# Routing from unnormalised rows: centred router weights, the norm's scale after the choice, and each batch placed during the next one's output

## What is computed

```python
def _layernorm(x, axis=-1, eps=1e-05):
    return (x - mean(x)) / sqrt(var(x) + eps)

def _L1_ffn_ref(x, Wr, W1, W2):            # E = 8 experts, cap = 256 tokens each
    probs = softmax(xf @ Wr)
    eidx = argmax(probs);  p_tok = probs[eidx]
    rank = (how many earlier tokens chose the same expert);  keep = rank < cap
    h = maximum(xe @ W1[e], 0);  ye = (h @ W2[e]) * p_tok * keep
...
x = x + 0.5 * _L0_ffn_ref(_layernorm(x), ...)      # twice, an attention between
x = x + 0.5 * _L1_ffn_ref(_layernorm(x), ...)      # stage 0
x = x + _L1_attn_ref(_layernorm(x), ...)
x = x + 0.5 * _L1_ffn_ref(_layernorm(x), ...)      # stage 1
```

## Time and profile before

| | us |
|---|---|
| median of 3 runs | 621.57 (620.26 to 624.51) |
| profiled execution, device time | 621.04 |
| its span, first to last instruction | 619.2 |
| busy in that span: PE, DVE, POOL, ACT | 505.4, 342.3, 243.5, 214.8 |

### The profile page before, as it was taken

The page is one execution under the profiler, slowest core; times in us unless marked ns, Lnnn a source line. Parts: engine busy times, 40 slices in busy tenths (PEclk is TensorE's granted clock), DMA queues, the critical chain, the costliest instruction groups (busy, mean ns, idle before and its releaser), DMA issues.

```text
span 619.2 us, 10399 instructions
## 1 busy us (share of the span) xinstructions
PE 505.4 (82%) x3827; PEld 322.3 (52%) x3827; DVE 342.3 (55%) x912; ACT 214.8 (35%) x298; POOL 243.5 (39%) x292
## 2 busy tenths in 40 slices
PE   1787787989999999987888878965887788788893
PEld 0664333434644644462467744962456566563692
DVE  5654585648487757751144760323696888842131
ACT  1346331644455455445643701202231311110120
POOL 5667464223342334235332467452220220323153
PEclk9998797989999999998999999997998989977997
DMA  7306999733263263225299523312756273110220
GB/s 261 146 23 198 311 279 298 195 117 95 69 188 96 62 158 118 58 45 155 71 174 217 165 86 111 94 40 72 201 183 187 74 201 111 54 51 35 86 63 10
DMA packets 73666, 79.85 MB, mean 129 GB/s; under 512 B 10946, under 2 KB 50499, under 8 KB 73360
## 3 DMA queue, kind: packets, MB, share of 16 engines
q1 hardware_dynamic: 70760, 73.15, 42.6%
q0 software_dynamic: 2560, 5.58, 2.6%
q10 hardware_dynamic: 296, 0.47, 0.2%
HBM read 44.07 MB, written 35.72 MB: 129 GB/s over the span
## 4 chain that ended last, share of the span: by engine, by line
PE 49%; DVE 17%; SPq 8%; DMA 7%; POOL 7%; issue 6%; ACT 5%; POOLq 0%; DVEq 0%; ACTq 0%
PE ps_accum L1505 15%; PE ps_pair L1505 15%; PE ps_max_pair L1505 13%; SPq L366 3%; POOL sb_rstd L583 2%; DVE sb_stats L1061 2%; DVE sb_work L1400 2%; DMA sb_v_next<-v_scr 2%; DVE sb_mpart L1164 2%; SPq L380 1%; SPq L402 1%; PE ps_turn L1513 1%; POOL xe_scr L603 1%; PE ps_max_pair L1513 1%; DVE sb_mv L1064 1%
## 5 line engine op out<-in xcount | busy, mean ns | idle before, releaser
L1164 DVE TENSOR_REDUCE sb_mpart<-ps_max_pair 128x4 f32<-128x512 f32 x132 | 88.0, 688 | 47.1 <-PE ps_max_pair L1505 46.7
L900 ACT ACTIVATE sb_work<-ps_pair 128x1024 f32<-128x1024 f32 x80 | 80.9, 1024 | 71.3 <-PE ps_pair L1505 70.5
L1505 PE MATMUL ps_max_pair<-sb_ring,sb_m_sets 128*128 128x512 f32 x146 | 64.8, 471 | 7.6 <-DVE sb_mpart L1164 4.6
L660 POOL TENSOR_SCALAR_AFFINE_SELECT sb_work<-sb_work 128x512 f32<-128x512 f32 (+1 forms) x48 | 37.7, 789 | 72.1 <-ACT sb_work L900 72.1
L1505 PE MATMUL ps_pair<-sb_ring,sb_xsets 128*128 128x512 f32 x160 | 58.7, 455 | 8.9 <-DMA sb_ring<-sb_qs 3.7
L1505 PE MATMUL ps_pair<-sb_ident_bf,sb_ones_bf 128*128 128x512 bf16 x185 | 50.6, 431 | 12.3 <-DMA sb_x<-y_scr 8.0
L1505 PE MATMUL ps_accum<-sb_work,sb_v_aug 128*32 128x128 f32 (+3 forms) x768 | 59.3, 408 | 1.1 <-POOL sb_work L660 1.1
L1505 PEld LDWEIGHTS ps_max_pair<-sb_ring,sb_m_sets 128*128 128x128 f32 x146 | 26.9, 191 | 45.1 <-DVE sb_mpart L1164 28.7
L1505 PEld LDWEIGHTS ps_pair<-sb_ring,sb_xsets 128*128 128x128 f32 x160 | 29.0, 200 | 22.6 <-DMA sb_ring<-sb_qs 7.1
L1400 DVE TENSOR_TENSOR sb_work<-ps_pair,sb_cst 128x1024 f32<-128x1024 f32 x32 | 37.5, 1214 | 2.6 <-PE ps_pair L1505 2.6
L1505 PEld LDWEIGHTS ps_pair<-sb_ident_bf,sb_ones_bf 128*128 128x128 bf16 x185 | 19.9, 110 | 36.3 <-issue 11.7
(11 more groups left out here) (251 smaller groups left out, 994.6 us busy)
## 6 DMA issues: line engine op xcount, KB each, us to landing
sb_expert_rows<-xe_scr SPq DMA_DIRECT2D x16, 258.0 KB, 2.8
sb_m_sets<-q_scr SPq DMA_DIRECT2D x16, 256.0 KB
sb_ka_stk<-mk_scr SPq DMA_DIRECT2D x4, 1024.0 KB
xe_scr<-sb_cst SPq DMA_DIRECT2D x4, 1024.0 KB, 12.8
sb_mw<-in_mw SPq DMA_DIRECT2D x16, 256.0 KB, 5.9
sb_ka_stk<-mk_scr SPq DMA_DIRECT2D x8, 512.0 KB
sb_xsets<-k_scr SPq DMA_DIRECT2D x15, 256.0 KB
q_scr<-sb_qs SPq DMA_DIRECT2D x12, 256.0 KB, 3.7
```

The costliest lines, as they stand in the source:

```text
L660: pool.affine_select(weights, weights, [[0, weights.shape[1]], [0, HL], [1, P]], ALU.is_ge, 0.0, base=0, channel_multiplier=-1).then_inc(s ...
L900: act.activation(unit_slots(i), pair[u % 2][:], ACT.Exp, scale=SCALE).then_inc(s["exp_done"], 1)
L1164: dve.tensor_reduce(mpart[:, m // NPAIR, m % NPAIR, :], max_banks[m % 2][:].rearrange("p (h k) -> p h k", h=HL), AX.X, ALU.max).then_inc(s ...
L1505: return pe.matmul(dst, lhsT, rhs, start=start, stop=stop, skip_group_check=True)
```

## The change

The router's product is made on raw rows. Since the norm takes the mean off each row and multiplies by one positive number per row, `norm(x) @ Wr = rstd * (x @ (Wr - column means of Wr))`: the weights are centred once at the start, the choice is made on the unscaled logits, and only the Exp gets logits multiplied by rstd (`scaled_logits`). The placed rows still hold normed values. In stage 0 a batch's logits go behind the first quarter of the next batch's output and its ranks behind the third; DVE chooses and places a batch in the same `after_attention(b)`, so ahead of the next batch's add; POOL scatters one batch earlier than before. `place` is put in another order (what needs no ranks comes first; the same lines go from further down, which is not shown), and the one-hot's f32 copy counts the semaphore too. The unread products are set anew, and now a part of them waits until the scatters have landed.

POOL, stage 0:

```diff
-            for b in range(2):
+            rsqrt(norm_second(B), 0)
+            for b in range(1, B):
+                scatter(0, b - 1, 0, 2)
                 rsqrt(norm_second(B + b), b % 2)
-            for b in range(2, B):
-                scatter(0, b - 2, 0, 2)
-                rsqrt(norm_second(B + b), b % 2)
-                scatter(0, b - 2, 2, NT)
-            for b in range(B - 2, B):
-                scatter(0, b)
+                scatter(0, b - 1, 2, NT)
+            scatter(0, B - 1)
```

ACT:

```diff
             def router_exp(r):
-                act.wait_ge(s["lg_sub"], r + 1)
-                act.activation(r8[1][:], r8[0][:], ACT.Exp).then_inc(s["lg_exp"], 1)
+                act.wait_ge(s["lg_scaled"], r + 1)
+                act.activation(r8[1][:], r8[1][:], ACT.Exp).then_inc(s["lg_exp"], 1)
...
             def after_attention(b):
-                if b:
-                    turned_full(B + b - 1, turn[0], xnT[(b - 1) % 2][:])
                 if b + 1 < B:
                     gelu(B + b + 1)
+                turned_full(B + b, turn[1], xnT[b % 2][:])
                 if b + 2 < B:
                     turned_high(B + b + 2)
-                if b:
-                    router_exp(b - 1)
-                    if b + 2 < B:
-                        ready(ACT.Gelu)
+                router_exp(b)
+                if b + 2 < B:
+                    ready(ACT.Gelu)
```

DVE:

```diff
+            def scaled_logits(r, norm):
+
+                dve.wait_ge(s["rstd"], norm + 1)
+                dve.tensor_tensor(r8[1][:], r8[0][:], rstd[r % B % 2][:].unsqueeze(2).broadcast_to([P, NT, E]),
+                                  ALU.mult).then_inc(s["lg_scaled"], 1)
+
...
             def place(r, b, bank, places):
+                dve.wait_ge(s["top_onehot"], 2 * r + 2)
+                dve.tensor_tensor(r8[5][:].rearrange("p t e -> p (t e)"), r8[3][:].rearrange("p t e -> p (t e)"),
+                                  const("slot_base"), ALU.mult).then_inc(s["rank_c"], 1)
+                dve.tensor_scalar(rows_out[r // B][b][:, :, ID], spare[:], float(-NTOK), None, ALU.add)
+                dve.wait_ge(s["rank_c"], 2 * r + 1)
+                dve.tensor_reduce(r1[5][:], r8[5][:], AX.X, ALU.add).then_inc(s["rank_d"], 1)
+                dve.wait_ge(s["lg_exp"], r + 1)
+                dve.tensor_reduce(r1[2][:], r8[1][:], AX.X, ALU.add).then_inc(s["top_sum"], 1)
+                dve.wait_ge(s["top_sum"], r + 1)
+                dve.reciprocal(r1[3][:], r1[2][:]).then_inc(s["top_rcp"], 1)
                 dve.wait_ge(s["rank_mm"], r + 1)
...
             def after_attention(b):
                 old = rows_out[0][b][:, :, OLD:RW]
                 ffn_x(B + b, x[b], old)
-                moments(norm_second(B + b), old, b % 2)
-                if b:
-                    choose(b - 1, accum[1])
-                normalise(norm_second(B + b), old, rows_out[0][b], b % 2)
+                n = norm_second(B + b)
+                moments(n, old, b % 2)
+                choose(b, accum[1])
+                normalise(n, old, rows_out[0][b], b % 2)
+                scaled_logits(b, n)
                 if b + 2 < B:
                     low(B + b + 2)
-                if b:
-                    place(b - 1, b - 1, accum[1], slot_all[:, NT * (b - 1):NT * b])
+                place(b, b, accum[1], slot_all[:, NT * b:NT * (b + 1)])
...
+            dve.wait_ge(s["wr_sum"], 1)
+            dve.scalar_tensor_tensor(out=wr_sb[:], in0=turn[1][:, 0:E], scalar=-1.0 / D, in1=wr_sb[:],
+                                     op0=ALU.mult, op1=ALU.add).then_inc(s["wr_mid"], 1)
...
             leave(B - 1)
+            choose(2 * B - 1, turn[1])
             normalise_exit(B - 1)
-            choose(2 * B - 1, turn[1])
+            scaled_logits(2 * B - 1, norm_of_exit(B - 1))
             place_exit(B - 1)
```

PE:

```diff
+                if b == 0:
+                    pe.wait_ge(s["loaded"], 16 * (LOADS - FIRST_LOADS))
+                    mm(turn[1][:, 0:E], const("ones"), wr_sb[:]).then_inc(s["wr_sum"], 1)
...
                 def route(i):
-                    if i == 1:
-                        if b + 1 < B:
-                            turned_first_read(f + 1)
-                        turn_second(f - 1, rows_out[0][b - 1])
-                    elif i == 2:
+                    if i == 0:
...
                         logits(b - 1, f - 1, accum[1], xnT[(b - 1) % 2])
+                    elif i == 2:
+                        ranks(b - 1, accum[1])
 
                 output(f, route if b else None)
                 if b + 1 < B:
                     hidden(f + 1)
+                else:
+                    stay_awake(4, pair[1][:, 0])
+                pe.wait_ge(s["ffn_x"], f + 1)
+                turn_tiles(turn[1], rows_out[0][b][:, :, OLD:RW]).then_inc(s["x2_mm"], 1)
                 if b + 2 < B:
                     turn_first(f + 2, xn_third[b + 2])
-                if b == B - 1:
-                    stay_awake(13, pair[1][:, 0])
-                if b:
-                    ranks(b - 1, accum[1])
...
-            stay_awake(4, pair[1][:, 0])
-            turn_second(2 * B - 1, rows_out[0][B - 1])
             stay_awake(2, pair[1][:, 0])
...
             pe.wait_ge(s["experts_loaded"], 16 * 2 * E)
+            stay_awake(8, pair[1][:, 0])
             pe.wait_ge(s["rank_j"], B)
-            stay_awake(32, pair[1][:, 0])
+            stay_awake(24, pair[1][:, 0])
+            pe.wait_ge(s["scattered"], 16 * NT * B)
+            stay_awake(14, pair[1][:, 0])
             experts(0)
...
-                turn_norm(norm_of_exit(b), rows_out[1][b])
+                turn_tiles(turn[1], rows_out[1][b][:, :, OLD:RW]).then_inc(s["x2_mm"], 1)
...
             project_out(B - 1)
-            stay_awake(27, pair[0][:, 0])
+            stay_awake(4, pair[0][:, 0])
             turn_exit(B - 1)
             stay_awake(2, pair[0][:, 0])
             logits(2 * B - 1, turned(norm_of_exit(B - 1)), turn[1], xnT[1])
             stay_awake(3, pair[0][:, 0])
             ranks(2 * B - 1, turn[1])
+            stay_awake(8, pair[0][:, 0])
             pe.wait_ge(s["rank_j"], 2 * B)
-            stay_awake(32, pair[1][:, 0])
+            stay_awake(24, pair[1][:, 0])
+            for left in sent[1]:
+                pe.wait_ge(left, 16 * NT * B // 2)
+            stay_awake(14, pair[1][:, 0])
             experts(1)
```

More of the change, by code:

```diff
@@ L97 @@
 max_t_evac st_mm exp_done late_zero pv_mm y_evac y_t rcp y_norm err err_pad ma_mm ma_masked ma_copied ma_zeroed
-kv_mm kv_evac ym_mm yar_mm yar_evac y_sum proj_mm attn_base attn_x lg_mm lg_max lg_sub lg_exp
+kv_mm kv_evac ym_mm yar_mm yar_evac y_sum proj_mm attn_base attn_x wr_sum wr_mid lg_mm lg_max lg_sub lg_scaled lg_exp
 top_cand top_max top_onehot top_sum top_rcp rank_mm rank_a rank_b rank_c rank_d rank_e rank_f rank_g
@@ L951, in _ @@
                 after_attention(b)
-            turned_full(2 * B - 1, turn[0], xnT[(B - 1) % 2][:])
-            router_exp(B - 1)
             act.wait_ge(s["scattered"], 16 * NT * B)
@@ L1110, in choose @@
                 dve.tensor_tensor(onehot_bf[:], r8[2][:], top, ALU.is_equal).then_inc(s["top_onehot"], 1)
-                dve.tensor_tensor(r8[3][:], r8[2][:], top, ALU.is_equal)
+                dve.tensor_tensor(r8[3][:], r8[2][:], top, ALU.is_equal).then_inc(s["top_onehot"], 1)
             def place(r, b, bank, places):
@@ L1121, in place @@
                 dve.tensor_tensor(r8[4][:], r8[4][:], r8[3][:], ALU.mult).then_inc(s["rank_c"], 1)
-                dve.tensor_tensor(r8[5][:].rearrange("p t e -> p (t e)"), r8[3][:].rearrange("p t e -> p (t e)"),
-                                  const("slot_base"), ALU.mult).then_inc(s["rank_c"], 1)
                 dve.wait_ge(s["rank_c"], 2 * r + 2)
                 dve.tensor_reduce(r1[4][:], r8[4][:], AX.X, ALU.add).then_inc(s["rank_d"], 1)
-                dve.tensor_reduce(r1[5][:], r8[5][:], AX.X, ALU.add).then_inc(s["rank_d"], 1)
                 dve.wait_ge(s["rank_d"], 2 * r + 2)
@@ L1130, in place @@
                 dve.tensor_tensor(r1[7][:], r1[4][:], r1[5][:], ALU.add).then_inc(s["rank_e"], 1)
-                dve.wait_ge(s["lg_exp"], r + 1)
-                dve.tensor_reduce(r1[2][:], r8[1][:], AX.X, ALU.add).then_inc(s["top_sum"], 1)
                 dve.wait_ge(s["rank_e"], 2 * r + 2)
                 dve.tensor_tensor(r1[7][:], r1[7][:], spare[:], ALU.subtract).then_inc(s["rank_f"], 1)
-                dve.wait_ge(s["top_sum"], r + 1)
-                dve.reciprocal(r1[3][:], r1[2][:]).then_inc(s["top_rcp"], 1)
                 dve.wait_ge(s["top_rcp"], r + 1)
@@ L1140, in place @@
                                          op0=ALU.mult, op1=ALU.mult)
-                dve.tensor_scalar(rows_out[r // B][b][:, :, ID], spare[:], float(-NTOK), None, ALU.add)
                 dve.wait_ge(s["rank_f"], r + 1)
@@ L1336, in _ @@
                 after_attention(b)
-            choose(B - 1, accum[1])
-            place(B - 1, B - 1, accum[1], slot_all[:, NT * (B - 1):NT * B])
```

(5 more changed lines are left out.)

## The result

On one chip the kernel after took 613.21 us (median of 4 runs, 612.66 to 616.18) and the kernel before 622.56 (4 runs): a ratio of 0.988, 95% interval 0.983 to 0.9929. A second comparison (10 and 30 runs) gave 613.83 against 621.19, 0.9902 with 0.9871 to 0.9933. The profiled execution after took 612.66 (a span of 610.9), 8.4 less than the profiled one before; forecast were 5.05 less, 616.0. So the medians differ by 9.3 and 7.4 us, at or a little above the 1% that a measurement can tell.

What follows compares the result with a forecast made beforehand. No single engine bounds the kernel; in the routing stages the chain does, in stage 0 also POOL's queue. 621.04 - 4.0 - 2.25 + 0.2 + 0.2 + 0.65 + 0.15 gives 616.0; own range 613.5 to 618.3, 8 in 10 612.5 to 620.4.

Steps and rivals of the forecast that it cites:

- Stage 1, -4.0 + 0.2: Routing at the linear attention's exit (554 to 577 us): places written at 561.9 instead of 565.89, -4.0; unread products +0.2.
- Stage 0, -2.25 + 0.2: Routing out of the second feed-forward (334 to 381 us): last scatter at 372.85 instead of 375.09, -2.25; unread products +0.2.
- its loop: Stage 0's pass from one batch's add to the next, turns through placing: 9.1 us, gone through three times.
- POOL's factor between the scatters: Stage 0, batch 2 and last batch: normalising waits for POOL's factor behind two scatters; batch 2's comes at 356.0.
- The added wait: Stage 0: choice and placing (2.3) stand ahead of the next batch's add; PE's next turn and output wait for it.
- Tables: Stage 0: Exp loads (1.28) run in ACT's idle time, way back hidden; rival: loads wait, total 619.7, chance 0.12.
- Linear attention, +0.65: Scaling (0.22) and longer placing (0.2) come three times between masks on DVE: 0 to 1.3, half taken, +0.65.
- "better" rival: Rival: the earlier start shifts the half-speed clock stretch (544.2 to 551.0) out of the last attention step; 612.9, chance 0.10.
- Centring, +0.15: First 40 us: one product of 8 columns and one small DVE instruction cost between 0 and 0.5, taken as 0.15.
- the tail, +0.2 in each stage: Ahead of the experts: 14 unread products end 3.02 after the scatters land, against 2.86 until rows are in: +0.2.
- The slower side: Rival: TensorE's clock falls to half around the logits and stays there through all unread products; 629.5, chance 0.04.

Runs made afterwards that it cites:

- stage0_only: The kernel after with stage 1 routing normalised rows in the order of before, centred weights and new placing order kept; 616.64 us, 0.9946 of before.
- the moved placing: The kernel after, but in stage 0 DVE places a batch behind the next batch's add instead of ahead of it; 614.37 us, 0.9888 of before.
- old_products: The kernel after with 32 unread products behind the last places as before, none behind the scatters' landing; 614.50 us, 0.9902 of before.
- no_products: The kernel after with all unread products ahead of the experts left out in both stages; 619.20 us, 0.9964 of before.
- four_look: The kernel before with 4 unread products instead of 27 ahead of stage 1's exit transposes, looked at once more; 619.66 us, 0.9982 of before.

## Why the prediction was right, and where it was off

The mechanism was right in both stages; the sum was 2.4 short by the segments, 2.0 of it in two terms (stage 0 and the linear attention). The first median, 613.21, lies 0.3 under the range that the forecast gave itself (613.5 to 618.3), the second, 613.83, just inside. That the total fits is not the proof, since the second interval holds the 5.05 of the forecast as well; the segments are.

- **Stage 1, -4.0 + 0.2.** Measured -4.2 and -4.1, or 3.6 to 3.7 less than the lowest stage 1 without raw rows (21.83 in stage0_only). Transposes 0.06 behind the add (551.02), the choice taking 1.11, normalising 1.03 to the next start, placing: each within 0.2 of its step. The scaling is 0.10 from start to start (555.58 to 555.68), below the 0.13 to 0.23 that I gave as bounds.
- **Stage 0, -2.25 + 0.2.** Measured -3.5: this is the term that was mis-sized, as the prediction feared, by its loop. With the 1.01 taken off by which the whole stage lay later, the second add started at 341.95 (forecast 342.3), the fourth at 358.94 (359.8), the places were written at 366.80 (368.05) and the last scatter went at 371.38 (372.85). So 0.35 came ahead of the second add, 0.5 in two passes (8.87 and 8.12 from add to add, forecast 9.1 and 8.4), 0.4 in the last batch's chain and 0.2 in the scatters' pace. Logits to choice took 0.99 to 1.07, not 1.14; scaling and low part 0.71, not 0.9; and for the last normalising I took its 1.33, though the next instruction starts 1.03 behind its start. Which part of the stage's edit (raw rows, earlier scatters) brings how much was not tried apart.
- **POOL's factor between the scatters.** I had it hold the normalising twice. With the shift taken off it comes 0.9 earlier than I said (356.14 - 1.01 = 355.13 against 356.0), since the scatters ahead of it start earlier too. The choice ends just behind it, normalising starts at 356.49, and so it holds nothing. How near that is, the moved placing shows.
- **The added wait.** The add does stand behind placing, and PE's next turn behind the add; that it would lengthen every pass was wrong, since PE has no sooner use for the add in the first two; only ahead of the last batch does PE idle for it, 1.33.
- **Tables.** Right: the load runs ahead of the operand in all three batches, and the way to Exp cost nothing while ACT had idle time to load in; with the load behind the wait, stage 0 was 5.6 longer. The Trainium skill (ScalarE: Activation LUTs, Table sets: the hidden batching unit) puts a load at about 2.7 us. This case's trace does not agree: its rows have 1.28, and the Exp starts 0.01 behind the load (337.61 + 1.28 = 338.89, 338.90).
- **Linear attention, +0.65.** Too much. Placing takes 2.27 instead of 2.12, with 0.10 of scaling 0.25 per batch, and the lowest of all spans are 71.79 with the change in it and 71.64 without: +0.15. The 1.8 gained in the first profile is the clock, as far as the profiles show: without the change this part also takes 71.6 to 71.7 in three profiles and 73.6 in two. The "better" rival thus showed in a profile, but as chance, not as the change's work.
- **Centring, +0.15, and the tail, +0.2 in each stage.** Neither can be told. From the last scatter's start to the expert rows' transposes before has 5.70 and 5.89, after 5.92 and 5.76. That the tail gains nothing was right, but the row it was read from (590 to 612 in the earlier trace rows) starts 13 us into the experts; old_products is what shows it.
- **The slower side.** The clock fell as that rival says (555.14, at 0.56) and recovered within the unread products. Without these it doesn't: in no_products it stays at 0.50 until 386.0 in stage 0, and in stage 1 the experts' first eight products take 3.78 as well.

With the terms as measured, -3.5 - 4.1 + 0.15 = -7.45, near the 7.4 between the medians of the second comparison (621.19 to 613.83).

## What to carry to other kernels

Size a chain by the distance from one start to the next, not by the instructions' durations: the next step can start sooner (1.03 behind a normalising that takes 1.33), and a loop repeats the error. Before pricing a wait that an edit adds, find the later of the two engines that meet there; and an instruction that is moved off a path can push another (here the moments, and so POOL's factor) onto it. What filling products are worth shows in the work behind them (some 5 us of experts here), so cut them only where that work now starts sooner. And where the times scatter as much as the gain, compare segments of several profiles.

## What was not expected of the hardware

- With PE idle for 4.15 us the clock was at half (0.51) for 13.8 us, though the 32 products from 564.95 on lie in that stretch too (four_look); with 2.04 idle us behind 32 products it was at 1.00 (old_products). After 13.3 idle us it stayed at 0.50 until 386.0, 6.7 us into the experts (no_products).
- An activation's table load doesn't wait for the semaphore that the activation waits for (336.97 against 340.20), and stays behind it as soon as the wait is an instruction of its own (337.61, with 3.33 idle ahead).
- Two profiles of one kernel place their clock falls differently (541.5 to 545.0 and 541.3 to 548.5 in the kernel after): the linear attention takes 71.85 in one and 73.73 in the other, so 1 to 2 us of any single profile here need not be the edit's.
